# The second loop of a two-layer network: loop heads in the middle of the work, and more of the dense expert ahead of the triangular solve

## The chip, the cores and the metric

The program runs on one core of one Trainium2 chip. The metric is the device time of one launch, in microseconds (us), as the median of several runs. Names of the engines: PE is TensorE (matrix products and transposes), DVE is VectorE, ACT is ScalarE, POOL is GpSimd, SP is the engine that issues transfers. A PE product of float32 operands is issued as two passes; "x8" in a row of the profile counts passes.

## What is computed

The input is 8 batches of 512 tokens with 128 features. Two layers run one after the other; each normalises its input and adds an attention-like block and a mixture of experts to it. The change touches the second layer only:

```
xn = layernorm(x)
x  = x + L1_attn_ref(xn, ...) + L1_ffn_ref(xn, ...)

L1_attn_ref:
    x = zrms(hidden, w_ln1);  qkvz = x @ W_qkvz;  q, k, v, z = split(qkvz)
    b, a = split(x @ W_ba);   beta = sigmoid(b);  g = -exp(A_log) * softplus(a + dt_bias)
    q, k, v = silu(causal_dwconv([q, k, v], conv_w))          # 4 taps, 2048 channels
    step: S = S * exp(g);  S = S + k (v - k S) beta;  o = q S  # over 512 tokens, 8 heads of 128 x 128
    core = rms(o) * gate_norm_w * silu(z);  h = resid + core @ W_out
    h + sum over the top 2 of 8 small experts of (silu(gate) * up) @ down
L1_ffn_ref:
    probs = softmax(x @ w_router);  top 2 of 8 experts
    out = sum_e probs_e * (gelu(x @ w1_e + b1_e) @ w2_e + b2_e)   # hidden width 512, all 8 experts computed
```

The recurrence over tokens is computed in four chunks of 128 tokens. For each chunk and head a 128 x 128 unit lower triangular system is inverted: first its 32 x 32 diagonal blocks, all of them at once, by substitution (this is the triangular solve), then the larger blocks by products.

## The kernel before, in words

A first loop of 8 iterations computes layer one for each batch, a second loop of 8 iterations (one batch each, b) computes layer two. In the second loop every engine runs its own instruction stream. One list, `schedule_l1`, gives the order of steps; each engine walks through it and emits what it has to do for a step, or nothing. Semaphores order the engines among each other, and within an engine the order of the list is kept strictly. The names of the steps:

- `qkv m` projects channel blocks m and m+1 (PE, L692) into banks 2 to 5 of PSUM and ACT copies them to the ring CV of four (L1014); `taps m` are six multiply-adds on DVE (L1519) with the older taps; `silu m` (ACT, L1021) writes the activated block and for m below 8 its square (L1026); `ssq m` sums the squares on PE (L716). Block m+4 needs the ring place of block m: its copy waits for that block's silu, its product for that block's taps.
- `gg`, `gc`: decay rates on DVE (L1498), their sums on PE (L700), a copy on DVE (L1504), and SP sends it to DRAM and back in four broadcasts (L418, L422) for `scan` (DVE, L1531). `stat` makes scales (L1536), `gam` exponentials (ACT, L1030, L1033) and products (POOL, L1165). `prep c` makes key products (PE, L729, banks 0 and 1 in turn) and multiplies them by the decays (DVE, L1562). `stat2` (L1549 to L1553) makes more scales, `wfT` transposes the dense router's weights (PE, DVE copy L1508).
- `sub 0` to `sub 3`: the triangular solve, 31 steps of two operations on DVE (L1575, L1577), each waiting for the one before. Then SP writes the result to DRAM and reads it back in another layout; `inv` (PE, ACT, DVE, POOL L1175) builds the larger blocks.
- `cz c`: the z projection (PE, L737, banks 0 and 1) and its silu (ACT, L1040); for c of 2 and 3 the result is stored over the solve's memory. `cv c`: v transposed and scaled (ACT, L1053).
- The dense expert: 32 steps f, four for each of 8 experts e. `fh f` (PE, L871) makes a 128 x 512 block of the hidden layer in PSUM bank HBANK[f], `gelu f` (ACT, L1100), `fo f` (PE, L881) adds its product to bank OBANK[e], and `facc e` (DVE, L1684) takes the finished expert out of that bank, so that the bank can be used again. Where HBANK is the same for f and f+1, `fh f+1` waits for `gelu f`.
- Steps of the tail: `moe1 p` are the four pairs of small experts (L921, L923, L927; DVE L1729, L1733; their down product L915, and `moe1_last`, L1739). Among them the next batch is begun: `gn`, `gx`, `gz`, `gT`, `gr`, `gzT`, `gba`, and `gend`, which makes the gates (L1482 to L1487) and the router's top 2 (L1447 to L1490) on DVE and their exponentials on ACT (L997 to L1003).

Ahead of the loop the tail's part for the first batch is emitted once. Each engine's loop head lies at the start of the list, between `gend` and `qkv 0`. The lines that set the placement of the dense expert:

```
HBANK = (7, 4, 5) + (7,) * 17 + (2,) * 12
OBANK = (6, 3, 6, 3, 6, 3, 5, 3)
```

## Time and profile before

| | us |
|---|---|
| median of 3 runs (3119.16 to 3141.93) | 3121.79 |
| the profiled execution, whole | 3141.66 |
| its span in the trace | 3139.9 |
| PE busy, weight loads busy | 2691.1, 1805.5 |
| DVE, ACT, POOL busy | 2042.6, 1185.7, 382.3 |

The first loop ends at about 1160 us of the span; the second fills the rest. The profiled execution was 20 us longer than the median. A row of the timeline reads: start in us, duration in us, engine, source line, operation, tensors written and read, shapes, count, and in brackets how long the engine had been idle before it and what ended that. PEclk is the clock granted to PE as a share of full speed; it has the levels 1.0 (2.4 GHz) and 0.5 (1.2 GHz). `arena` is the name of nearly all of the working memory and `bank` that of all PSUM banks, so a row is identified by its line.

### The profile page before, as it was taken

What the parts mean: (1) busy time and instruction counts of PE and PEld (TensorE: products, weight loads), DVE (VectorE), ACT (ScalarE), POOL (GpSimd) and SP (SyncE); (2) the same over time, 40 slices, a digit from 0 to 9 for tenths busy, and PEclk for the clock granted to TensorE, in tenths of its full rate; (3) what the DMA queues carried; (4) which work ended last, traced back from release to release, by engine and by line L of the source; (5) the groups of instructions that cost most, each with busy time, mean ns of one, the idle gap of its engine ahead of it and who ended that gap; (6) DMA issues with size and microseconds to landing.
All of it is one profiled execution on the core that took longest, in us unless ns stands there. A gap on an engine that the chain in (4) does not pass through costs nothing.

```text
span 3139.9 us, 48523 instructions
## 1 busy us (share of the span) xinstructions
PE 2691.1 (86%) x15020; PEld 1805.5 (58%) x15020; DVE 2042.6 (65%) x6346; ACT 1185.7 (38%) x2170; POOL 382.3 (12%) x284
## 2 busy tenths in 40 slices
PE   2888888888888867997997897898898898898898
PEld 1434343343433425784785685585596595586587
DVE  4757666585766748558558557657656756845845
ACT  0132231313223125445445444444444444544543
POOL 0000000000000002122112122021120220221211
PEclk8888878897898967998998998997998898899799
DMA  5020101102011121101101101101201201100110
GB/s 139 10 38 7 33 14 25 35 5 37 12 28 21 18 51 41 48 11 58 48 11 58 48 11 49 57 8 48 61 1 55 54 8 55 43 19 28 54 34 15
DMA packets 133697, 109.63 MB, mean 35 GB/s; under 512 B 76968, under 2 KB 117488, under 8 KB 132944
## 3 DMA queue, kind: packets, MB, share of 16 engines
q1 hardware_dynamic: 130192, 100.01, 12.7%
q10 hardware_dynamic: 3264, 6.82, 0.6%
q8 instruction: 100, 1.64, 0.2%
q14 instruction: 141, 1.16, 0.1%
HBM read 86.62 MB, written 20.19 MB: 34 GB/s over the span
## 4 chain that ended last, share of the span: by engine, by line
PE 62%; issue 18%; DVE 11%; DMA 3%; ACT 3%; SPq 2%; POOL 1%; DVEq 0%; ACTq 0%; POOLq 0%
PE bank L871 7%; PE bank L881 7%; PE bank L459 5%; DMA arena<-scrk 3%; DVE arena L1519 3%; PE bank L716 2%; PE bank L610 2%; PE bank L737 2%; PE bank L819 2%; PE bank L555 2%; PE bank L782 2%; PE bank L777 2%; PE bank L765 2%; PE bank L540 2%; PE bank L769 2%
## 5 line engine op out<-in xcount | busy, mean ns | idle before, releaser
L881 PEld LDWEIGHTS bank<-wring,arena 128*128 128x128 f32 x2048 | 269.1, 192 | 109.5 <-issue 107.2
L871 PE MATMUL bank<-arena,wring 128*128 128x512 f32 x512 | 294.8, 666 | 25.9 <-ACT arena L1100 25.9
L1100 ACT ACTIVATE arena<-bank,w_b 128x512 f32<-128x512 f32 x256 | 175.1, 687 | 274.2 <-PE bank L871 273.9
L1519 DVE SCALAR_TENSOR_TENSOR arena<-bank,w_convw,arena 128x511 f32<-128x511 f32 (+2 forms) x384 | 254.8, 740 | 34.6 <-ACT arena L1014 34.5
L881 PE MATMUL bank<-wring,arena 128*128 128x128 f32 x2048 | 271.1, 276 | 0.0
L973 ACT ACTIVATE arena<-bank 128x512 f32<-128x512 f32 x136 | 81.4, 599 | 494.7 <-PE bank L540 441.9
L459 PE MATMUL bank<-w_ident,arena 128*128 128x128 f32 (+2 forms) x1164 | 178.5, 293 | 86.4 <-DVE arena L1266 35.7
L1372 DVE CUSTOM_DVE_ANT_0 bank<-bank,arena 128x128 f32<-128x128 f32 (+3 forms) x512 | 249.2, 492 | 0.0
L982 ACT ACTIVATE arena<-bank 128x512 f32<-128x512 f32 (+1 forms) x384 | 171.1, 535 | 148.9 <-PE bank L597 147.1
L459 PEld LDWEIGHTS bank<-w_ident,arena 128*128 128x128 f32 (+2 forms) x1164 | 135.9, 141 | 118.6 <-issue 66.6
L692 PE MATMUL bank<-arena,w_Wqkvz 128*128 128x512 f32 x256 | 152.7, 733 | 45.0 <-DVE arena L1519 26.1
L1066 ACT ACTIVATE arena<-bank 128x512 f32<-128x512 f32 (+1 forms) x256 | 118.7, 488 | 136.2 <-PE bank L777 69.3
L570 PE MATMUL bank<-arena 48*128 48x128 bf16 (+3 forms) x512 | 110.7, 317 | 64.7 <-DVE arena L1372 36.0
L555 PE MATMUL bank<-arena 128*128 128x128 f32 x1088 | 161.7, 293 | 2.7 <-DVE arena L1357 2.7
L1684 DVE SCALAR_TENSOR_TENSOR arena<-bank,arena 128x128 f32<-128x128 f32 x224 | 63.1, 344 | 154.5 <-PE bank L881 152.7
L540 PE MATMUL bank<-arena 128*128 128x512 f32 x272 | 156.3, 659 | 8.1 <-ACT arena L973 8.1
L326 DVE TENSOR_TENSOR tick<-nhalf 128x1 f32<-128x1 f32 x600 | 94.1, 157 | 93.0 <-PE bank L570 86.4
L543 PE MATMUL bank<-arena 128*128 128x512 f32 x272 | 152.2, 644 | 0.0
L570 PEld LDWEIGHTS bank<-arena 48*128 48x128 bf16 x512 | 34.1, 93 | 200.5 <-DVE arena L1372 92.3
L555 PEld LDWEIGHTS bank<-arena 128*128 128x128 f32 x1088 | 135.6, 196 | 22.8 <-issue 11.3
L1175 POOL TENSOR_TENSOR arena<-arena,w_blk 128x512 f32<-128x512 f32 x64 | 79.8, 1268 | 509.5 <-PE bank L765 358.8
L1165 POOL TENSOR_TENSOR arena<-arena 128x512 f32<-128x512 f32 x64 | 92.3, 1475 | 352.2 <-ACT arena L1033 224.6
(273 smaller groups left out, 5209.3 us busy)
## 6 DMA issues: line engine op xcount, KB each, us to landing
wring<-in_w_last SPq DMA_DIRECT2D x64, 512.0 KB, 3.3
arena<-scrg SPq DMA_DIRECT2D x32, 512.0 KB, 5.4
arena<-scrq SPq DMA_DIRECT2D x108, 64.0 KB
arena<-scrk SPq DMA_DIRECT2D x108, 64.0 KB
scrn<-arena SPq DMA_DIRECT2D x64, 64.0 KB, 1.9
arena<-scrn SPq DMA_DIRECT2D x8, 512.0 KB, 3.6
scrx<-arena SPq DMA_DIRECT2D x8, 512.0 KB, 2.6
arena<-scrx SPq DMA_DIRECT2D x64, 64.0 KB, 2.1
```

Source lines behind the costliest of these rows:

```text
L459: return nc.tensor.transpose(dst, src, W["ident"][0:k, 0:k])
L540: mm(bk[:, :], W["gate0"][:, p, :] if p < PR0 else W["sg"][:], xnT, start=True, stop=True).then_inc(*s["p_gate"].up)
L543: mm(bk[:, :], W["up0"][:, p, :] if p < PR0 else W["su"][:], xnT, start=True, stop=True).then_inc(*s["p_up"].up)
L555: last = mm(bank[7][:, t * P:(t + 1) * P], HID[:, p % 2, t * P:(t + 1) * P], W["down0"][:, p, :] if p < PR0 else W["sd"][:], start=(p == 0 ...
L570: mm(bk[:, 0:w], QS[o:o + KROWS, h // 2, qt * P:(qt + 1) * P], KS[o:o + KROWS, h // 2, 0:w], start=True, stop=True, tile_position=(o, 0)). ...
L692: mm(bk[:, :], W["Wqkvz"][:, m * P:(m + 1) * P], zT, start=True, stop=True).then_inc(*s["p_qkv"].up)
L871: mm(bank[HBANK[f]][:, :], wring[:, e % 2, k * P:(k + 1) * P], xn1T, start=True, stop=True).then_inc(*s["p_fh"].up)
L881: last = mm(bank[OBANK[e]][:, t * P:(t + 1) * P], GH[:, f % 2, t * P:(t + 1) * P], wring[:, e % 2, FC * P + k * D:FC * P + (k + 1) * D], s ...
L982: fn(PT[:, slot, col:col + w], bank[SBANK[n % 4]][:, 0:w], ACT.Exp, scale=float(HD) ** -0.5).then_inc(*s["a_p"].up)
L1100: fn(GH[:, f % 2, :], bank[HBANK[f]][:, :], ACT.Gelu_apprx_tanh, bias=W["b1"][:, f:f + 1]).then_inc(*s["a_gh"].up)
L1372: v.tensor_tensor_reduce(bk[:, 0:w], bk[:, 0:w], W["maskq"][:, S - w:S], 1.0, PAD, ALU.add, ALU.max, mx[:, col:col + 1]).then_inc(*s["v_ma ...
L1519: ins = v.scalar_tensor_tensor(out=cv[:, k:S], in0=bank[2 + m % 4][:, 0:S - k], scalar=W["convw"][:, m, 3 - k:4 - k], in1=cv[:, k:S], op0= ...
```

## The change

**The order.** The list from `qkv 0` to the end of the solve is new, and HBANK and OBANK with it:

```diff
-HBANK = (7, 4, 5) + (7,) * 17 + (2,) * 12
-OBANK = (6, 3, 6, 3, 6, 3, 5, 3)
+HBANK = (1, 7, 7, 4, 5) + (7,) * 15 + (2,) * 12
+OBANK = (6, 6, 2, 3, 6, 3, 5, 3)
...
+    order = [("qkv", 0), ("fh", 0), ("gelu", 0), ("fh", 1), ("gelu", 1), ("taps", 0), ("gg",), ("qkv", 2), ("silu", 0)]
+    order += [("fo", 0), ("fo", 1), ("taps", 2), ("qkv", 4), ("gc",), ("silu", 2), ("taps", 4), ("ssq", 0)]
     order += [("qkv", 6), ("silu", 4), ("taps", 6), ("ssq", 2), ("silu", 6), ("scan", 0), ("ssq", 4), ("ssq", 6), ("stat",)]
...
+    order += [("scan", 1), ("fh", 2), ("fh", 3), ("fh", 4), ("gam",), ("prep", 0), ("gelu", 2), ("fo", 2), ("prep", 1), ("gelu", 3)]
+    order += [("fh", 5), ("fo", 3), ("qkv", 8), ("gelu", 4), ("prep", 2), ("gelu", 5), ("prep", 3), ("facc", 0), ("fo", 4), ("rr",)]
+    order += [("qkv", 10), ("fo", 5), ("taps", 8), ("fh", 6), ("gelu", 6), ("fh", 7), ("gelu", 7), ("taps", 10), ("silu", 8), ("fo", 6)]
+    order += [("qkv", 12), ("taps", 12), ("silu", 10), ("fo", 7), ("qkv", 14), ("taps", 14), ("silu", 12), ("silu", 14)]
+    made[:] = 8, 8
+    order += [("cz", 0), ("cz", 1), ("sub", 0)] + ffn(4) + [("sub", 1), ("facc", 1)] + ffn(3) + [("sub", 2), ("facc", 2)] + ffn(3)
+    order += [("sub", 3), ("facc", 3), ("stat2",)] + ffn(1) + [("wfT",), ("cz", 2), ("cz", 3), ("cv", 0)] + ffn(1) + ffn_rest() + [("facc", 4)]
```

Before, `fh 0` to `fh 3` stood ahead of `sub 0`, and `fh 4` to `fh 19` beside the solve with `facc 0` and `facc 1`; `wfT` and `stat2` stood between `taps 14` and `sub 0`.

**The tail.** `gend` is split in three: `gfe` (exponential and softmax of the dense router) ahead of `moe1 3`, `gab` (the gates) and `gpick` (the top 2) after it and ahead of `moe1_last`. Three small operations on beta and a move from the gates into `gg`. The down products are steps of their own, one of them placed after `gzT` and one after `gba`.

**The loop heads.** PE, ACT and DVE emit the part of the list ahead of a turning point once before the loop; the loop then holds the rest of an iteration and the first part of the next, 7 times, and the last rest follows behind it. PE turns ahead of `cz 0`:

```diff
+            turn = L1.index(("cz", 0))
+            ahead_of_loop(gT, gr, gzT, gba, first_part)
+            with pe.Fori(0, LOOPS - 1) as b:
+                second_part(b, 0)
+                first_part(b, 1)
+            out_of_loop(second_part, LOOPS - 1)
```

ACT turns in the same way ahead of `("qkv", 10)`, DVE behind `("sub", 3)`. POOL and SP keep theirs. SP loads the first two experts of the next batch at its end and no longer at its start. Some waits follow the new banks: `fo 4` waits for `facc 0`, `cz 2` for the copy of `wfT`, and `wfT` for the second silu of `cz 1`.

In the engines' own order it looks so. PE from the first key products on; bank 0 and 1 are the key products (`prep`), bank 6 is `fo`, bank 7 `fh`, bank 2 and 3 `qkv 8`. Before:

```order
L729 MATMUL bank0<-arena 128x256 x2
L676 REGISTER_ALU
L729 MATMUL bank1<-arena 128x256 x2
L676 REGISTER_ALU
L729 MATMUL bank0<-arena 128x256 x2
L676 REGISTER_ALU
L729 MATMUL bank1<-arena 128x256 x2
L876 ISA
L881 MATMUL bank6<-wring,arena 128x128 x4
L692 MATMUL bank2<-arena,w_Wqkvz 128x512
L692 MATMUL bank3<-arena,w_Wqkvz 128x512
```

and now, where the rows with bank 6 are `fo 2` and `fo 3`:

```order
L738 MATMUL bank0<-arena 128x256 x2
L738 MATMUL bank1<-arena 128x256 x2
L894 MATMUL bank6<-wring,arena 128x128 x4
L738 MATMUL bank0<-arena 128x256 x2
L738 MATMUL bank1<-arena 128x256 x2
L884 MATMUL bank7<-arena,wring 128x512
L894 MATMUL bank6<-wring,arena 128x128 x4
L700 MATMUL bank2<-arena,w_Wqkvz 128x512
L700 MATMUL bank3<-arena,w_Wqkvz 128x512
```

An output product of the dense expert now stands between the first and the second pair of key products; before, the first one stood behind both pairs.

ACT around the copies of `qkv 10` into CV; L1014 and L1042 are these copies, L1100 and L1128 the gelu, L1021 and L1049 the silu. Before:

```order
L1014 ACTIVATE arena<-bank5,w_convw 128x512
L1095 REGISTER_ALU
L1100 ACTIVATE arena<-bank7,w_b1 128x512
L1019 REGISTER_ALU
L1021 ACT_TABLE_LOAD
L1021 ACTIVATE arena<-arena 128x512
L1019 REGISTER_ALU
L1021 ACTIVATE arena<-arena 128x512
L1011 REGISTER_ALU
L1014 ACTIVATE arena<-bank2,w_convw 128x512
```

and now (the rest of an iteration behind the end of the loop):

```order
L1159 COMPARE_AND_BRANCH
L1042 ACTIVATE arena<-bank4,w_convw 128x512
L1042 ACTIVATE arena<-bank5,w_convw 128x512
L1128 ACTIVATE arena<-bank7,w_b1 128x512 x2
L1049 ACT_TABLE_LOAD
L1049 ACTIVATE arena<-arena 128x512 x2
L1042 ACTIVATE arena<-bank2,w_convw 128x512
```

Two gelus, `gelu 6` and `gelu 7`, stand ahead of `silu 8` where one stood, and the loop's branch ahead of all of them.

DVE at the end of the solve, whose steps are L1575 and L1577 before and L1630 and L1632 now; L1684 and L1739 are `facc`. Before:

```order
L1258 REGISTER_ALU
L1577 TENSOR_TENSOR arena<-arena 128x31
L1675 REGISTER_ALU
L1684 SCALAR_TENSOR_TENSOR arena<-bank6,arena 128x128 x4
L1675 REGISTER_ALU
L1684 SCALAR_TENSOR_TENSOR arena<-bank3,arena 128x128 x4
L1675 REGISTER_ALU
L1684 SCALAR_TENSOR_TENSOR arena<-bank6,arena 128x128 x4
```

and now, where L1817 is the loop:

```order
L1632 TENSOR_TENSOR arena<-arena 128x31
L1817 REGISTER_ALU
L1817 COMPARE_AND_BRANCH
L1739 SCALAR_TENSOR_TENSOR arena<-bank,arena 128x128 x4
L1604 SCALAR_TENSOR_TENSOR arena<-arena 128x32
L1605 TENSOR_SCALAR arena<-arena 128x32
L1607 TENSOR_SCALAR arena<-arena 128x16
L1608 TENSOR_TENSOR arena<-arena 128x16
L1563 COPY arena<-bank 8x512
```

Three `facc` followed the last step of the solve; now the branch, one `facc`, `stat2` (L1604 to L1608) and the copy of `wfT` (L1563) follow it, in that order.

## Rows read from the trace of the kernel before

**Rows 1.** The page's first line.

```profile
span 3139.9 us, 48523 instructions
```

**Rows 2.** The last addition of an iteration (L1739), by its line.

```profile
L1739 DVE TENSOR_TENSOR arena<-arena,bank x8: 686/689/690, 1423.5 to 3135.4; 128x512 f32<-128x512 f32 x8
```

**Rows 3.** Busy time by stretch: the solve's, and the rest to `gend`.

```profile
1733.30:1777.70 44.40, 41.28 (x193) 26.79 (x194) 28.50 (x85) 21.71 (x32) 2.50 (x2) 0.96 0.25 72
1777.70:1908.90 131.20, 127.10 (x888) 109.88 (x886) 72.88 (x237) 51.46 (x107) 25.13 (x21) 0.96 0.04 11
```

**Rows 4.** Timeline where one iteration ends and the next begins.

```profile
1663.78 0.69 DVE L1733 TENSOR_TENSOR arena<-arena,bank 128x512 f32<-128x512 f32 x1
...
1666.51 0.18 DVE L1482 TENSOR_TENSOR arena<-bank,w_dtb 128x32 f32<-128x32 f32 x1
...
1668.28 0.37 DVE L1243 MAX8 top<-pad 128x8 f32<-128x8 f32 x4
...
1668.55 5.39 PE L692 MATMUL bank<-arena,w_Wqkvz 128*128 128x512 f32 x8 [2.68 <-issue]
...
1670.69 0.69 ACT L1014 ACTIVATE arena<-bank,w_convw 128x512 f32<-128x512 f32 x1 [1.75 <-PE bank L692]
...
1673.64 4.03 DVE L1519 SCALAR_TENSOR_TENSOR arena<-bank,w_convw,arena 128x511 f32<-128x511 f32 x6 [3.56 <-ACT arena L1014]
```

**Rows 5.** Timeline of DVE at its head in the first loop.

```profile
462.70 0.68 DVE L1238 TENSOR_TENSOR arena<-arena 32x512 bf16<-32x512 f32 x1
465.69 0.69 DVE L1389 COPY arena<-bank 128x512 f32<-128x512 f32 x1 [2.30 <-issue]
```

**Rows 6.** Timeline: the decay sums leave DVE, and the scan.

```profile
1679.05 0.28 DVE L1504 COPY arena<-bank 32x127 f32<-32x127 f32 x1 [1.06 <-PE bank L459]
...
1691.06 4.55 DVE L1531 TENSOR_TENSOR_SCAN arena<-arena,w_floor 128x512 f32<-128x512 f32 x4
```

**Rows 7.** DMA issues of 1682.0 to 1682.7: median us to landing last.

```profile
arena<-scrg SPq DMA_DIRECT2D x2, 512.0 KB, 6.2
```

**Rows 8.** Timeline of the key products and the gelus beside them.

```profile
1704.35 1.28 ACT L1100 ACT_TABLE_LOAD   x1
1704.90 0.73 PEld L729 LDWEIGHTS bank<-arena 128*128 128x128 f32 x4 [3.18 <-DVE arena L1562]
...
1705.64 1.27 ACT L1100 ACTIVATE arena<-bank,w_b 128x512 f32<-128x512 f32 x2
...
1712.40 5.11 DVE L1562 TENSOR_TENSOR arena<-bank,arena 128x512 f32<-128x512 f32 x8 [2.98 <-PE bank L729]
...
1713.06 1.05 PE L881 MATMUL bank<-wring,arena 128*128 128x128 f32 x8
```

**Rows 9.** Timeline of the later taps and the silu beside them.

```profile
1717.42 15.83 DVE L1519 SCALAR_TENSOR_TENSOR arena<-bank,w_convw,arena 128x511 f32<-128x511 f32 x24
...
1720.82 1.28 ACT L1021 ACTIVATE arena<-arena 128x512 f32<-128x512 f32 x2
```

**Rows 10.** Timeline of the solve: its start, one expert step, its end.

```profile
1733.99 2.50 POOL L1175 TENSOR_TENSOR arena<-arena,w_blk 128x512 f32<-128x512 f32 x2 [20.11 <-ACT arena L1021]
1734.02 1.27 DVE L1553 TENSOR_TENSOR arena<-arena 128x16 f32<-128x16 f32 x1
...
1735.44 0.91 DVE L1569 MEMSET arena<- 128x1024 f32 x1 [0.16 <-issue]
...
1743.33 1.12 PE L871 MATMUL bank<-arena,wring 128*128 128x512 f32 x2 [1.52 <-ACT arena L1100]
...
1744.49 0.69 ACT L1100 ACTIVATE arena<-bank,w_b 128x512 f32<-128x512 f32 x1 [1.22 <-PE bank L871]
...
1762.25 1.13 DVE L1684 SCALAR_TENSOR_TENSOR arena<-bank,arena 128x128 f32<-128x128 f32 x4
1766.26 3.94 PE L737 MATMUL bank<-w_Wqkvz,arena 128*128 128x512 f32 x8
...
1777.90 1.13 DVE L1684 SCALAR_TENSOR_TENSOR arena<-bank,arena 128x128 f32<-128x128 f32 x4 [10.31 <-PE bank L881]
```

328 lines of the change are left out of this document (183 added, 145 removed).

## The prediction, made before the changed kernel was run

> **What bounds the kernel now.** I read the page's first line for the span [rows 1], then the last addition of each iteration by its line. Its eight starts lie 1711.9 us apart in seven periods, so an iteration of the second loop takes 244.6 us [rows 2]; the first loop isn't touched. Then I cut one iteration into stretches. From the inversion's products to the end PE is busy for 127 of 131 us [rows 3]: that part is PE's, and the change leaves its order alone but for the last few steps. So everything is decided between the last small expert (DVE's L1733) and the inversion's start, in three places.
>
> First, the seam between two iterations [rows 4]. DVE ends L1733 at 1664.47 and starts the first taps at 1673.64, 9.2 us later. The view names ACT's copy as what ended its last wait, but that copy was over at 1671.38, 2.3 us before. DVE's last work was over at 1670.08, and the gap behind it is 3.56 us; PE shows 2.68 us before L692 with nothing that it waited for. The same kind of gap, 2.30 us, stands at DVE's loop head in the first loop, where little else goes on [rows 5]. These are the heads.
>
> Second, the taps. From 1673.64 to 1733.25 DVE works nearly without a pause: the scan starts 17.4 us after the first taps [rows 4, 6], the last eight products of key and decay at 1712.40, and taps 8 to 14 fill 15.8 us [rows 8, 9]. DVE, not PE, sets when the solve can start.
>
> Third, the solve: DVE runs it from 1735.44 to 1762.25, 26.8 us with two `facc` in it. But the inversion starts only at 1777.7, with the last `fo`: DVE then has waited 10.31 us for PE [rows 10]. An expert step takes 0.69 + 1.22 = 1.91 us there. So PE's sixteen steps are late here, and not the solve.
>
> **The change part by part.** I write t for the time since the first taps of an iteration. Before: `taps 8` at 43.8, end of `taps 14` at 59.6, inversion at 59.6 + 44.45.
>
> *The seam.* No head is left in it. After L1733 DVE does the gates (from 1666.51, three operations, 0.6 us), the top 2 (from 1668.28 to 1670.08, 1.8 us) and the last addition (0.69 us) [rows 2, 4]: 3.1 us. ACT has two short exponentials, a table load (1.28 us [rows 8]) and a logarithm before its first copy of 0.69 us, about 3.4 us in all; PE's first product is issued right behind its last down product. I take 3.5 us, so 5.7 us are saved at each of seven seams: 39.9 us. Bounds: 2.6 (if only the head's idle 2.7 us of PE goes) and 6.1.
>
> *The decay sums.* Their copy to DRAM now stands behind `taps 2`: at t = 4.0 + 1.0 (`gg` with three more operations) + 4.0, ending at 9.3. From that copy to the last broadcast it takes 1682.2 + 6.2 - 1679.3 = 9.1 us [rows 6, 7], so the scan can't start before t = 18.4, where it started at 17.4. Cost 1.0 us (0 to 1.3). The two new gelus and their two table loads lie on ACT beside `taps 0`, and PE's `fh 0` to `fo 1` fill its pauses: 0 us.
>
> *`fo 2` between the key products.* Before, PE took up the third key product as soon as DVE freed its bank, at 1704.90 [rows 8]. Now it stands behind `fo 2`, which waits for `gelu 2`; ACT reaches that after its exponentials at 1704.35, plus 1.28 of table load and 0.64 of gelu, so 1706.3. `fo 2` then takes 0.9 us at PE's full clock and about twice that at the lower one (1.05 with its tail in [rows 8]). The third product is there at 1708.0 to 1709.7 where DVE could take it at 1706.1. Behind it the row of work (`fh 5`, `fo 3`, `qkv 8`) is as long as the one that made DVE wait 2.98 us. Cost 0.8 to 2.5 us; I take 1.5, since PE stands idle ahead of it and the clock tends to be low after that.
>
> *`facc 0` ahead of `taps 8`*: 1.13 us of DVE [rows 10], on the path. It isn't saved later, since the solve still holds two of its kind.
>
> *The copies for `taps 12`.* Let s be the start of `taps 8`. PE waits with `fo 4` for `facc 0`, that is until s; then `fo 4` 0.9, `qkv 10` 1.7, `fo 5` 0.9, `fh 6` 1.1 until its result: `gelu 6` from s + 4.7. `fh 7` has the same bank, so it follows at s + 5.5, `gelu 7` ends at s + 7.3, table load to s + 8.6, `silu 8` to s + 9.9 (1.28 [rows 9]), first copy to s + 10.6. DVE wants it at s + 8.0. What was hidden, since one gelu stood there and PE was early, is now 2.6 us late; `taps 14` has its copies in time. I take 2.9 (1.5 to 5.0; the upper end is PE at its lower clock).
>
> Sum up to the end of `taps 14`: 1.0 + 1.5 + 1.15 + 2.9 = 6.55 us later in t, in each of eight iterations: 52.4 us lost.
>
> *The solve and what follows it.* From the end of `taps 14`: the solve 26.8 us at once (the copy and `stat2` are gone from its front). POOL's two products, 1.25 us each, fall beside its first steps instead of beside `stat2`, where one small operation of 16 columns took 1.27 [rows 10] and one of 32 columns elsewhere takes 0.18 [rows 4]; 1.1 us (0 to 2.5). Then DVE's head, 3.0 us (2.3 [rows 5] to 3.6 [rows 4]), `facc 3` 1.1, `stat2` 0.6, copy of `wfT` 0.7: 33.3. Only then may `cz 2` start: both `cz` 4.6 us until their last silu, `cv 0` 1.6, table load 1.3, `gelu 19` 0.7, `fo 19` 0.9, pauses 0.6: 43.0 where it was 44.45. PE's eleven steps from `fh 8` end at about 26, so the four that were taken out of this stretch gain little: DVE's late head takes PE's place. Gain 1.45 us, eight times 11.6; the first and the last iteration have no head there, 2 x 3.0 = 6.0 more. Bounds per iteration: 3.5 gained, 2.5 lost. The heads of PE (before `cz 0`, which must wait for ACT's `silu 14` anyway) and ACT (before `qkv 10`, where it idles) I cost at nothing; without that cover each would be some 3 us.
>
> SP's two loads at the end of an iteration are transfers of the next experts 0 and 1, wanted only behind `qkv 0`, and are issued 20 us ahead: 0.
>
> Sum: 52.4 - 39.9 - 11.6 - 6.0 = -5.1 us. The profiled execution would take 3136.6; it was 20 us above the median, so I put the forecast at 3121.8 - 5 = 3117 us.
>
> **Two rules of the Trainium skill.** The page "Advanced Engine Details and Errata", section Control Flow Timing, gives about 108 ns for a compare-and-branch; "Runtime: NRT & Kernel Launch", section Instruction fetch mechanics, says that a taken branch to a target outside the fetched window stalls. The gaps of 2.3 to 3.6 us stand with the second. The page "SBUF — State Buffer", section on its two sides, says that a DVE operation with two SBUF inputs and a GpSimd operation exclude each other for a whole instruction; by that all of POOL's 2.5 us would be lost to the solve, and the sum would be an estimated +6 us in place of -5.
>
> **Rivals.** (a) The placements are absorbed: `fo 2` and the copies for `taps 12` come in time, because PE and ACT run earlier against DVE than I count. For it: ACT is busy for 28.5 of 44.4 us in the solve's stretch and for 51.5 of 131.2 behind it [rows 3], so it has room. Against: both orders are strict, and the steps were counted from rows. Without the 1.5 and the 2.9 us the sum is -5.1 - 35.2 = -40: 3081 us; with the solve's part at its better bound, 3062.
> (b) Slower: PE's lower clock. PE now stands still ahead of `fo 4` and for six us ahead of `cz 2`; in the kernel before, the eight passes of L692 behind a pause of 2.68 us took 5.39 us [rows 4], where those of `cz` behind another took 3.94 [rows 10]. If each of the two chains pays 2.5 us more, in every iteration, the sum is +35 us: 3157. It decides from about 4.5 us an iteration on.
> (c) The seam's gap isn't the head but something else that stays, as a branch of 0.1 us would have it. Then each seam saves 3.5 us less (+24.5) and DVE's turn after the solve costs nothing (-18): +1.4, 3123.
>
> **How the numbers follow.** Forecast 0.45, (a) 0.30, (b) 0.20, (c) 0.05. The forecast's own range is 3092 to 3150, from its bounds taken half together. 1% is 31 us, about what can be told from no change. Faster by more: 0.30; within: 0.50; slower by more: 0.20. The range over the cases is 3070 to 3158.
>
> **What would show it.** After: seven seams of 3.5 us from DVE's last L1733 to the first taps; no idle of 3 us there on PE. A wait of about 2.6 us of DVE before `taps 12`, ended by ACT's copy. Before the third key product, PE waiting for a gelu. After the solve an idle of 3 us on DVE, then PE waiting some 6 us for the copy of `wfT`, and no 10 us wait of DVE for the last `fo`. It is wrong if the seam saves under 4 us, or if DVE's taps run through without a gap.

## The result, and the profile after

The changed kernel took 3171.09 us (median of 4 runs, 3168.62 to 3178.63), the kernel before 3126.78 us beside it (3119.16 to 3141.93): a ratio of 1.014, 95% interval 1.0095 to 1.0184. A second measurement, on one chip with three of the experiments, gave 3175.54 us against 3139.60 us, ratio 1.011 (1.0071 to 1.0148). The change makes the kernel slower by 1.1 to 1.4%. The forecast of 3117 us had the wrong sign, and 3171 lies above its range, which ended at 3158. The two profiled executions that are compared below are 30 us apart (3141.66 and 3172.09), the medians 44 us and 36 us: the profiled execution of the kernel before was as long as the longest of its four runs, though near the medians of its later ones.

The page of the changed kernel, first the span and then the busy times of the engines:

```profile
span 3170.3 us, 48083 instructions
...
PE 2686.2 (85%) x15020; PEld 1806.1 (57%) x15020; DVE 2045.0 (65%) x6343; ACT 1205.0 (38%) x2194; POOL 382.0 (12%) x284
```

PE and DVE have as much to do as before (2691.1 and 2042.6). Only ACT has more, 1205.0 us where it had 1185.7, with 138 loads of its function table of 1.28 us each, where it had 114. The span is 30.4 us longer than that of [rows 1]. So on PE and DVE the change added waiting and not work. The last additions of the iterations, by their line, tell how much of it an iteration takes (they answer to [rows 2]):

```profile
L1794 DVE TENSOR_TENSOR arena<-arena,bank x8: 678/681/683, 1436.7 to 3166.7; 128x512 f32<-128x512 f32 x8
```

Seven periods take 3166.7 - 1436.7 = 1730.0 us, so 247.1 us for an iteration where it was 244.6. The measure for all experiments below is this period, since the first loop, which the change leaves alone, differs from one profiled execution to the next: the first taps of the second loop start at 1188.3 us in the kernel before, at 1194.5 in the changed one, and between 1183.8 and 1209.7 in the experiments. A kernel's own period differed by 0.4 to 0.6 us between its two profiled executions (runs 8 and the changed kernel), so smaller differences than that tell nothing.

**The seam.** The timeline of the changed kernel at the end of an iteration, as in [rows 4]; L1788 is the last small expert, L1794 the last addition, L1574 the taps:

```profile
1682.07 0.69 DVE L1788 TENSOR_TENSOR arena<-arena,bank 128x512 f32<-128x512 f32 x1
...
1683.99 1.88 PE L700 MATMUL bank<-arena,w_Wqkvz 128*128 128x512 f32 x4
...
1684.93 0.68 DVE L1794 TENSOR_TENSOR arena<-arena,bank 128x512 f32<-128x512 f32 x1
...
1685.83 4.17 DVE L1574 SCALAR_TENSOR_TENSOR arena<-bank,w_convw,arena 128x511 f32<-128x511 f32 x6 [0.22 <-ACT arena L1042]
```

From the end of L1788 at 1682.76 to the first taps at 1685.83 it is 3.1 us, where it was 9.2. PE starts the next projections, without a pause, while DVE still picks the top 2. This part of the change does what was expected.

**The key products.** The timeline from `prep 0` to `prep 2` of that iteration; L1617 is DVE's product of key and decay, L894 `fo`, L738 the key products, L1128 the gelu:

```profile
1716.94 2.45 DVE L1617 TENSOR_TENSOR arena<-bank,arena 128x512 f32<-128x512 f32 x4
1717.05 0.63 ACT L1061 ACTIVATE arena<-arena 128x512 f32<-128x512 f32 x1 [1.28 <-DVE arena L1586]
1717.70 1.28 ACT L1128 ACT_TABLE_LOAD   x1
1719.00 1.26 ACT L1128 ACTIVATE arena<-bank,w_b 128x512 f32<-128x512 f32 x2
1719.74 2.08 PE L894 MATMUL bank<-wring,arena 128*128 128x128 f32 x8 [5.49 <-ACT arena L1128]
...
1723.56 1.29 DVE L1617 TENSOR_TENSOR arena<-bank,arena 128x512 f32<-128x512 f32 x2 [4.16 <-PE bank L738]
...
1729.84 5.00 DVE L1617 TENSOR_TENSOR arena<-bank,arena 128x512 f32<-128x512 f32 x8 [3.28 <-PE bank L738]
```

PE waits 5.49 us for `gelu 2`, then needs 2.08 us for eight passes that took 1.05 in [rows 8], and DVE stands still for 4.16 us where it had worked on. The later wait of 3.28 is the old one of 2.98. The gelu itself comes when the prediction said, 2.7 us after the start of DVE's first product of key and decay (1719.63 after 1716.94; forecast 1706.3 after 1703.59). In the mean of eight iterations DVE's products of key and decay take 17.5 us from start to end, 12.6 before.

**The later taps.** The same iteration; L1737 is `facc 0`:

```profile
1734.75 1.12 DVE L1737 TENSOR_SCALAR arena<-bank,arena 128x128 f32<-128x128 f32 x4
...
1736.01 2.05 PE L894 MATMUL bank<-wring,arena 128*128 128x128 f32 x8 [2.50 <-DVE arena L1737]
...
1740.40 4.23 DVE L1574 SCALAR_TENSOR_TENSOR arena<-bank,w_convw,arena 128x511 f32<-128x511 f32 x6 [0.60 <-ACT arena L1042]
...
1748.03 7.96 DVE L1574 SCALAR_TENSOR_TENSOR arena<-bank,w_convw,arena 128x511 f32<-128x511 f32 x12 [3.40 <-ACT arena L1042]
```

In [rows 9] the 24 operations of `taps 8` to `taps 14` ran in one piece. Now there are waits of 0.60 and 3.40 us in them, for ACT's copies. PE ran `fo 4` in 2.05 us again, not in 1.05.

**The solve, its start.** DVE's first steps (L1630, L1632) and POOL's two products (L1221), which fell on `stat2` in [rows 10]:

```profile
1756.16 0.91 DVE L1624 MEMSET arena<- 128x1024 f32 x1 [0.16 <-issue]
1756.74 2.49 POOL L1221 TENSOR_TENSOR arena<-arena,w_blk 128x512 f32<-128x512 f32 x2 [29.51 <-ACT arena L1049]
...
1757.29 0.76 DVE L1630 TENSOR_TENSOR arena<-arena 128x31 f32<-128x31 f32 x1
1758.08 1.19 DVE L1632 TENSOR_TENSOR arena<-arena 128x31 f32<-128x31 f32 x1
1759.30 0.22 DVE L1630 TENSOR_TENSOR arena<-arena 128x60 f32<-128x60 f32 x1
```

**Its end.** L1739 is `facc 3`, L1563 the copy of `wfT`, L748 `cz 2` and `cz 3`, the last row the last `facc` ahead of the inversion:

```profile
1787.43 1.12 DVE L1739 SCALAR_TENSOR_TENSOR arena<-bank,arena 128x128 f32<-128x128 f32 x4 [2.88 <-issue]
...
1788.82 0.67 DVE L1563 COPY arena<-bank 8x512 f32<-8x512 f32 x1
...
1789.55 5.82 PE L748 MATMUL bank<-w_Wqkvz,arena 128*128 128x512 f32 x8 [6.23 <-DVE arena L1563]
...
1800.71 1.13 DVE L1739 SCALAR_TENSOR_TENSOR arena<-bank,arena 128x128 f32<-128x128 f32 x4 [11.22 <-PE bank L894]
```

DVE's head is the gap of 2.88 us that no other engine ended. PE waits 6.23 us for the copy of `wfT` behind it. `cz 2` and `cz 3` take 5.82 us where these products took 3.94 in [rows 10], and DVE waits longer for the last `fo` than before (11.22 against 10.31).

**The clock.** Busy time by stretch for five stretches of that iteration; the columns are the stretch, its length, busy us and count of PE, weight loads, DVE, ACT and POOL, then the granted clock as a share of 2.4 GHz, the DMA share and GB/s:

```profile
1718.00:1726.00 8.00, 6.26 (x18) 5.09 (x19) 3.42 (x7) 2.25 (x3) 8.00 (x5) 0.57 0.00 0
1734.00:1742.00 8.00, 5.99 (x22) 4.01 (x22) 7.29 (x15) 1.37 (x2) 0.00 (x0) 0.79 0.34 61
1755.00:1764.00 9.00, 5.82 (x7) 2.15 (x8) 8.15 (x21) 5.40 (x8) 2.49 (x2) 0.62 0.01 2
1786.00:1794.00 8.00, 4.45 (x6) 1.81 (x6) 2.06 (x9) 2.48 (x3) 0.00 (x0) 0.57 0.59 132
1810.00:1818.00 8.00, 8.00 (x44) 7.88 (x43) 1.62 (x4) 2.39 (x4) 0.00 (x0) 0.57 0.01 2
```

PE runs for most of four of them at the lower level, 1.2 GHz (0.57 and 0.62), and for some two fifths of the second (0.79). The first four hold the four long waits of PE: for `gelu 2`, for `facc 0`, for the silu ahead of `cz 1`, and for the copy of `wfT`. In the fifth PE is busy all the time: it is the inversion, ten us in, and PE is the bound there.

The kernel before is not free of this. In the iteration that the forecast read, the stretches that answer to the first four have clocks of 0.79, 1.00, 0.62 and 1.00. PE waited for the copy of `wfT` too, but ahead of the solve, and the eight passes of `cz 0` and `cz 1` behind that wait took 5.30 us. And in this iteration, though in no other of the eight, the inversion too ran at half clock for a stretch (a row of the timeline, then, in a view of its own, the stretch that answers to the fifth above):

```profile
1733.88 5.30 PE L737 MATMUL bank<-w_Wqkvz,arena 128*128 128x512 f32 x8 [6.68 <-DVE arena L1508]
```

```profile
1788.00:1796.00 8.00, 8.00 (x43) 7.88 (x43) 1.12 (x4) 2.39 (x4) 0.00 (x0) 0.57 0.01 2
```

Over the second loop, from its first taps to its last addition, PE has half clock for 335 us before and for 330 us in the changed kernel, and stands still for 211 and 243 us. So the change added no half clock in sum. It moved it: in all eight iterations of the changed kernel some of it lies in the inversion, which PE bounds, and before in one of eight. Before, most of it lay in the taps and at the start of the solve, where DVE sets the time.

### The profile page after: what moved, and what is told of

The parts are those of the page before. It is cut to its first block, busy times and chain, and to the rows that moved or that the text cites. A ratio compares the mean times of both kernels' runs of the same rounds, so it can differ in the third digit from the quotient of the medians.

```text
span 3170.3 us, 48083 instructions
## 1 busy us (share of the span) xinstructions
PE 2686.2 (85%) x15020; PEld 1806.1 (57%) x15020; DVE 2045.0 (65%) x6343; ACT 1205.0 (38%) x2194; POOL 382.0 (12%) x284
## 4 chain that ended last, share of the span: by engine, by line
PE 52%; issue 17%; DVE 16%; DMA 6%; ACT 4%; SPq 3%; POOL 1%; DVEq 0%; ACTq 0%; POOLq 0%
PE bank L470 5%; PE bank L894 4%; PE bank L884 4%; DMA arena<-scrk 4%; DVE arena L1632 3%; DVE arena L1630 3%; PE bank L830 2%; PE bank L566 2%; PE bank L793 2%; PE bank L621 2%; PE bank L788 2%; PE bank L776 2%; PE bank L551 2%; PE bank L780 2%; DVE arena L1574 2%
## 5 line engine op out<-in xcount | busy, mean ns | idle before, releaser
L894 PEld LDWEIGHTS bank<-wring,arena 128*128 128x128 f32 x2048 | 276.4, 199 | 187.1 <-issue 125.2
L894 PE MATMUL bank<-wring,arena 128*128 128x128 f32 x2048 | 283.6, 285 | 74.9 <-ACT arena L1128 54.9
L1574 DVE SCALAR_TENSOR_TENSOR arena<-bank,w_convw,arena 128x511 f32<-128x511 f32 (+2 forms) x384 | 257.2, 738 | 32.8 <-ACT arena L1042 31.8
L1128 ACT ACTIVATE arena<-bank,w_b 128x512 f32<-128x512 f32 x256 | 173.3, 687 | 252.1 <-PE bank L884 251.7
L748 PE MATMUL bank<-w_Wqkvz,arena 128*128 128x512 f32 x128 | 90.9, 861 | 93.6 <-ACT arena L1068 48.6
L1739 DVE SCALAR_TENSOR_TENSOR arena<-bank,arena 128x128 f32<-128x128 f32 x224 | 63.1, 344 | 147.0 <-PE bank L894 125.9
L566 PEld LDWEIGHTS bank<-arena 128*128 128x128 f32 x1088 | 135.9, 196 | 23.1 <-issue 12.6
L1221 POOL TENSOR_TENSOR arena<-arena,w_blk 128x512 f32<-128x512 f32 x64 | 79.7, 1267 | 574.0 <-PE bank L776 344.8
L884 PEld LDWEIGHTS bank<-arena,wring 128*128 128x128 f32 x512 | 91.1, 210 | 92.0 <-ACT arena L1128 46.7
```

The costliest lines, as they stand in the source:

```text
L566: last = mm(bank[7][:, t * P:(t + 1) * P], HID[:, p % 2, t * P:(t + 1) * P], W["down0"][:, p, :] if p < PR0 else W["sd"][:], start=(p == 0 ...
L884: mm(bank[HBANK[f]][:, :], wring[:, e % 2, k * P:(k + 1) * P], xn1T, start=True, stop=True).then_inc(*s["p_fh"].up)
L894: last = mm(bank[OBANK[e]][:, t * P:(t + 1) * P], GH[:, f % 2, t * P:(t + 1) * P], wring[:, e % 2, FC * P + k * D:FC * P + (k + 1) * D], s ...
L1128: fn(GH[:, f % 2, :], bank[HBANK[f]][:, :], ACT.Gelu_apprx_tanh, bias=W["b1"][:, f:f + 1]).then_inc(*s["a_gh"].up)
L1574: ins = v.scalar_tensor_tensor(out=cv[:, k:S], in0=bank[2 + m % 4][:, 0:S - k], scalar=W["convw"][:, m, 3 - k:4 - k], in1=cv[:, k:S], op0= ...
```

## The experiments

All times are medians; the ratio is to the kernel before, run beside it on the same chip. "Period" is the mean of seven in the profiled execution. "End of taps" is the end of `taps 14` since the first taps, "inversion" its first copy since the first taps, and "rest" from there to the start of DVE's last product for the small experts, each a mean over eight iterations. "Steps ahead" in runs 8 and 11 to 13 are steps of the dense expert moved ahead of the solve, beyond those of the kernel before.

| kernel | us | ratio (95%) | period | end of taps | inversion | rest |
|---|---|---|---|---|---|---|
| before | 3126.78 | 1 | 244.6 | 60.8 | 107.0 | 127.5 |
| changed | 3171.09 | 1.014 (1.0095 to 1.0184) | 247.1 | 69.1 | 113.5 | 129.4 |
| changed, again | 3175.54 | 1.011 (1.0071 to 1.0148) | 247.7 | 68.9 | 113.3 | 129.7 |
| 1 new heads, old order | 3110.77 | 0.988 (0.9836 to 0.9926) | 238.6 | 61.6 | 107.5 | 127.4 |
| 2 new order, heads at the start | 3160.44 | 1.004 (1.0019 to 1.0059) | 245.1 | 69.4 | 110.9 | 127.5 |
| 3 DVE's head behind `wfT` | 3156.28 | 1.003 (0.9996 to 1.0055) | 244.7 | 69.1 | 111.0 | 129.7 |
| 4 filled wait ahead of `cz 2` | 3161.22 | 1.005 (1.0027 to 1.0077) | 245.6 | 68.8 | 112.8 | 128.1 |
| 5 silu first | 3152.54 | 1.004 (1.0005 to 1.0068) | 244.4 | 66.7 | 111.8 | 128.3 |
| 6 `fo 2` behind | 3147.30 | 1.002 (0.9995 to 1.0046) | 243.8 | 66.7 | 111.5 | 127.8 |
| 7 all of 3, 5 and 6 | 3107.19 | 0.988 (0.9829 to 0.994) | 237.5 | 63.9 | 106.1 | 127.2 |
| 8 two steps ahead | 3098.69 | 0.986 (0.9794 to 0.9917) | 237.0 | 60.5 | 104.6 | 128.1 |
| 8 again | 3102.81 | 0.988 (0.9818 to 0.9942) | 237.4 | 60.4 | 104.7 | 128.3 |
| 9 old order, heads at the start | 3131.30 | 0.997 (0.9931 to 1.0005) | 242.3 | 62.0 | 108.1 | 127.8 |
| 10 four waits filled | 3125.28 | 0.995 (0.9907 to 0.9985) | 241.8 | 65.4 | 109.1 | 128.7 |
| 11 three steps ahead | 3115.55 | 0.991 (0.9873 to 0.9955) | 241.1 | 60.2 | 107.7 | 128.9 |
| 12 three steps, DVE's head late | 3085.29 | 0.982 (0.976 to 0.9884) | 235.7 | 60.1 | 103.8 | 127.9 |
| 13 two steps, DVE's head late | 3073.40 | 0.976 (0.9698 to 0.9828) | 235.1 | 60.8 | 103.8 | 127.4 |

Beside the experiments the kernel before ran 82 times more, in four groups with medians of 3146.63, 3143.23, 3139.60 and 3145.74 us and single runs from 3117.58 to 3168.43: two of the three runs behind the forecast were among its quickest. The ratios are taken within a group.

### 1 and 9: the heads and the tail without the new order

Run 1 is the changed kernel with the old list, its banks and its waits:

```diff
-    order = [("qkv", 0), ("fh", 0), ("gelu", 0), ("fh", 1), ("gelu", 1), ("taps", 0), ("gg",), ("qkv", 2), ("silu", 0)]
+    order = [("qkv", 0), ("taps", 0), ("gg",), ("qkv", 2), ("silu", 0), ("gc",), ("taps", 2), ("qkv", 4), ("silu", 2), ("taps", 4), ("ssq", 0)]
...
-HBANK = (1, 7, 7, 4, 5) + (7,) * 15 + (2,) * 12
-OBANK = (6, 6, 2, 3, 6, 3, 5, 3)
+HBANK = (7, 4, 5) + (7,) * 17 + (2,) * 12
+OBANK = (6, 3, 6, 3, 6, 3, 5, 3)
```

> The changed kernel with the list from qkv 0 to the solve, HBANK, OBANK and the waits that go with them as they were before; heads, tail and loads of the first experts as changed. The trace after shows 6.9 us less at each of seven seams. Theory H (the heads pay, the order costs): the DVE head behind sub 3 falls into DVE's wait of some 10 us for the last fo, the others into idle time too, so the gain is about 7 x 6.9 = 48 us: 3079 us where before takes 3127, and no half clock behind the inversion's start. Rival R (a head costs wherever it stands, and the half clock comes from the peeled loop, not from the order): 3120 to 3160 us, with DVE late behind the solve.

Run 9 has the three turning points at the start of that list besides:

```diff
-            turn = L1.index(("cz", 0))
+            turn = 0
...
-            turn = L1.index(("qkv", 10))
+            turn = 0
...
-            turn = L1.index(("sub", 3)) + 1
+            turn = 0
```

> The old order as in the run with the new heads alone (238.6 us an iteration), but all three turning points at the start of the list: the changed tail by itself. With the new order the same edit cost 2.9 us at each seam (6.7 instead of 3.8 from the last product of the small experts to the first taps; 9.85 before the change). Theory: half of what the seam gained came from the split of the gates and the top 2 in the tail and half from the heads: seam 6.7, iteration 241.5 us, ratio to before 0.988 + 0.007 = 0.995. Rival: the heads were worth all 6.1 us: seam 9.8, iteration 244.6.

Run 1 took 238.6 us an iteration, 5.9 less than before, and 8.5 less than the changed kernel. So the heads and the tail together are the gain, and the order, with its banks and waits, is the whole loss: it costs 8.5 us an iteration, and what the heads and the tail win covers 5.9 of it. The last additions of run 1, by their line:

```profile
L1788 DVE TENSOR_TENSOR arena<-arena,bank x8: 680/680/681, 1436.8 to 3107.2; 128x512 f32<-128x512 f32 x8
```

Run 9 took 242.3 us. From the last product of the small experts to the first taps (start to start) it is 9.85 us before, 6.37 in run 9 and 3.76 in run 1. So of the 6.1 us that the seam gained, 3.5 come from the split of the gates and the top 2 in the tail and 2.6 from the heads: near the theory that was put down for run 9, and not its rival. By the whole period the tail gave 2.3 us and the heads 3.7. In run 1 DVE's head stands behind the solve too (3.06 us of idle time that no engine ended), and still the inversion starts 107.5 us after the first taps, 107.0 before: the copy of `wfT`, which PE wants, is ahead of the solve there.

### 2 and 3: where DVE's head stands

Run 2 is the changed kernel with the three turning points at the start of the list, as in run 9. Run 3 moves one of them:

```diff
-            turn = L1.index(("sub", 3)) + 1
+            turn = L1.index(("wfT",)) + 1
```

> The changed kernel with all three turning points at the start of the list, so the heads of PE, ACT and DVE lie between gpick and qkv 0 again. Theory H: seven seams longer by 6 us (+42), DVE's 2.9 us behind the solve saved seven times (-20), and PE then waits 3.3 us and not 6.2 ahead of cz 2, which may or may not bring the clock back (0 to -39): 3154 to 3193 us where the changed kernel takes 3171. Rival R (the heads' places are indifferent): 3171 within 5.

> The changed kernel with only DVE's turning point moved from behind sub 3 to behind the copy of wfT, where DVE waits 11.2 us for the last fo. Theory H: cz 2 starts 2.9 us earlier in seven iterations, 20 us, and the head costs nothing where it stands: 3151 us. If PE's shorter wait ahead of cz 2 also keeps the clock up for cz 2, cz 3 and the inversion's first products, up to 39 us more: 3112. Rival: the last fo sets the inversion anyway: 3171.

In run 2 the seam is 2.9 us longer and the inversion starts 2.6 us earlier since the first taps; the rest is 127.5 us and not 129.4, so the period is 245.1, 2.0 less than with the heads in their new places. In run 3 the inversion starts 2.5 us earlier and the period is 244.7, 2.5 less. In this order the head behind `sub 3` costs nearly what its gap is (2.88 us). Run 3 has both gains and still is not faster than the kernel before. Its "rest" is 129.7, as in the changed kernel, so the shorter wait ahead of `cz 2` (3.4 us and not 6.2; `cz 2` starts 2.2 us earlier) did not bring the clock back. The further 39 us of the expectation did not come.

### 4 and 10: is it the waits or the clock?

Run 4 gives PE five products in its wait for the copy of `wfT`, run 10 gives it products in four waits. Nothing reads their results.

```diff
                         if c == 2:
+                            if i == 0:
+                                need("a_sz", 4)
+                                for _ in range(5):
+                                    mm(bank[1][:, :], W["Wqkvz"][:, 0:P], W["Wqkvz"][:, 0:4 * P], start=True, stop=True)
                             need("v_wfT", 1)
```

> The changed kernel with five extra products of 128 x 512 on PE in its wait for the copy of wfT ahead of cz 2; their result in bank 1 is overwritten and never read. They fill 4.7 of 6.2 us and add no work elsewhere. Theory C (PE's standing still ahead of cz 2 brings the half clock in cz 2, cz 3 and the inversion's first products): cz 2 and cz 3 take 4.0 us again and not 5.8, and the stretch from the inversion's start to the last addition 129.7 and not 132.5 us: 8 x 4.7 = 38 us less, 3133. Rival (the half clock there follows from something else, or only shifts): 3171 within 10, with the half clock as before.

> The changed kernel with extra products of 128 x 512 in four of PE's waits: five ahead of fo 2, two ahead of fo 4, five ahead of the second product of cz in the wait for silu 14, five ahead of cz 2. Their results lie in banks 2, 7, 7 and 1, are overwritten and never read. Theory C (PE's standing still is what brings the half clock): the stretches at half clock at t = 32 to 39, 49 to 53, 70 to 77, 101 to 108 and 125 to 132 shrink or vanish, cz 2 and cz 3 take 4.0 us instead of 5.7, the inversion's start to the last product of the small experts 127.4 instead of 129.4, and the taps end 2 to 3 us earlier: 241 us an iteration instead of 247.1. Rival (the waits alone cost, the clock only follows them): 247 or more, since some of the extra products end after the wait that they fill.

Run 10 adds 69 us to PE's busy time (2755.6 against 2686.2) and in its profiled execution, the longest of its ten, takes 5.8 us less an iteration than the changed kernel beside it (241.8 against 247.7), a ratio of 0.995 where that has 1.011. Its busy time by stretch, for the five stretches that answer to those above (the same times since the first taps; same columns):

```profile
1725.00:1733.00 8.00, 6.78 (x33) 4.86 (x33) 3.62 (x6) 2.81 (x5) 8.00 (x5) 1.00 0.11 19
1741.00:1749.00 8.00, 7.14 (x30) 3.92 (x29) 6.64 (x11) 4.42 (x6) 0.00 (x0) 1.00 0.46 140
1762.00:1771.00 9.00, 7.17 (x35) 4.65 (x35) 8.12 (x26) 4.19 (x6) 0.00 (x0) 1.00 0.01 2
1793.00:1801.00 8.00, 7.18 (x25) 3.71 (x23) 0.00 (x0) 5.17 (x10) 0.00 (x0) 0.79 0.47 107
1817.00:1825.00 8.00, 8.00 (x72) 8.00 (x71) 3.29 (x6) 2.88 (x5) 1.57 (x2) 0.98 0.00 0
```

and its last additions, by their line:

```profile
L1806 DVE TENSOR_TENSOR arena<-arena,bank x8: 680/680/683, 1448.8 to 3141.6; 128x512 f32<-128x512 f32 x8
```

The clock is up in the first three, and PE gets through 72 passes in the last where it got through 44. The end of the taps comes 3.5 us earlier, `cz 2` to its end takes 5.1 us and not 5.7. Over the second loop half clock is granted for 174 us, where the changed kernel beside it has 328. So the waits of the changed kernel cost twice: for their own length, and for the half clock of the work behind them; the second price is at least the 5.8 us an iteration that more work on the same engine gives back. It is not what the change added: the kernel before has as much half clock (335 us), and it was not run with such products, so that it may well gain by them too. How much of the 8.5 us that the order costs is clock stays open, but for the rest behind the inversion's start (see below). In run 4, with one wait filled, the period was 1.5 to 2.0 us below that of the changed kernel (247.1 and 247.7), where 4.7 were expected: the low clock in `cz 2` and in the inversion came a little later and was shorter (7.3 us of the rest at half clock, 9.4 and 9.8 in the changed kernel), but it came. What decides whether a given wait brings it, these runs don't show; in run 10 four of the eight iterations have no half clock between 30 and 110 us after their first taps, and the other four have it once there.

### 5 and 6: the two placements that make DVE wait

```diff
-    order += [("qkv", 10), ("fo", 5), ("taps", 8), ("fh", 6), ("gelu", 6), ("fh", 7), ("gelu", 7), ("taps", 10), ("silu", 8), ("fo", 6)]
-    order += [("qkv", 12), ("taps", 12), ("silu", 10), ("fo", 7), ("qkv", 14), ("taps", 14), ("silu", 12), ("silu", 14)]
+    order += [("qkv", 10), ("fo", 5), ("taps", 8), ("silu", 8), ("qkv", 12), ("fh", 6), ("taps", 10), ("silu", 10), ("qkv", 14), ("taps", 12)]
+    order += [("gelu", 6), ("fh", 7), ("gelu", 7), ("fo", 6), ("silu", 12), ("fo", 7), ("taps", 14), ("silu", 14)]
```

> The changed kernel with silu 8, qkv 12, silu 10 and qkv 14 ahead of gelu 6 and gelu 7 (fh 7, fo 6 and fo 7 follow them). In the changed kernel DVE waits 0.6 us before taps 10 and 3.4 us before taps 12 for ACT's copies. Theory: these waits go and nothing else takes their place, so the end of taps 14 comes 4 us earlier and an iteration takes 243.1 us where the changed kernel has 247.1 (mean of seven periods); ratio to before 1.014 - 0.010 = 1.004. Rival (the clock: PE stands still longer in this stretch and pays it back at half clock in cz, the dense expert or the inversion): 245 to 247 us.

```diff
-    order += [("scan", 1), ("fh", 2), ("fh", 3), ("fh", 4), ("gam",), ("prep", 0), ("gelu", 2), ("fo", 2), ("prep", 1), ("gelu", 3)]
-    order += [("fh", 5), ("fo", 3), ("qkv", 8), ("gelu", 4), ("prep", 2), ("gelu", 5), ("prep", 3), ("facc", 0), ("fo", 4), ("rr",)]
+    order += [("scan", 1), ("fh", 2), ("fh", 3), ("fh", 4), ("gam",), ("prep", 0), ("prep", 1), ("gelu", 2), ("fo", 2), ("gelu", 3)]
+    order += [("qkv", 8), ("prep", 2), ("fh", 5), ("fo", 3), ("gelu", 4), ("gelu", 5), ("prep", 3), ("facc", 0), ("fo", 4), ("rr",)]
```

> The changed kernel with fo 2 behind the second pair of key products and fh 5 and fo 3 behind the third. In the changed kernel DVE waits 4.16, 0.42 and 3.28 us among the products of key and decay; the kernel before waits once, 2.98 us. Theory: PE's wait of 5.5 us for gelu 2 no longer stands ahead of the third key product; from prep 0 to the end of prep 3 it takes 13 us again and not 17.5: 4.5 us an iteration, 242.6 where the changed kernel has 247.1, ratio to before 1.002. Rival: fo 3 and gelu 5 are later now and delay facc 0, which gives 2 us or more of it back: 245.

Run 5 took 2.7 us less an iteration than the changed kernel and run 6 3.3 us; 4.0 and 4.5 were expected. In run 5 it takes 17.1 us from `taps 8` to the end of `taps 14`, 19.8 in the changed kernel and 15.8 before: of the 4.0 us two pauses of 0.7 and 0.6 us stay, ahead of `taps 10` and behind its first operation; the one ahead of `taps 12` is gone. PE's own head, hidden in the changed kernel, shows in this run: 1.8 to 2.6 us of idle time ahead of `cz 0` that no engine ended. In run 6 the waits among the products of key and decay are 0.97, 2.19 and 0.99 us in place of 4.16, 0.42 and 3.28; the kernel before had two, 0.77 and 2.98, and not the one that the expectation names (the timeline of run 6, DVE alone):

```profile
1701.83 2.61 DVE L1617 TENSOR_TENSOR arena<-bank,arena 128x512 f32<-128x512 f32 x4 [0.97 <-PE bank L738]
1706.63 2.48 DVE L1617 TENSOR_TENSOR arena<-bank,arena 128x512 f32<-128x512 f32 x4 [2.19 <-PE bank L738]
1710.11 2.48 DVE L1617 TENSOR_TENSOR arena<-bank,arena 128x512 f32<-128x512 f32 x4 [0.99 <-PE bank L738]
```

Its `taps 12` waits longer in return (from `taps 10` to `taps 12` it is 7.9 us, 7.4 in the changed kernel). Each of the two placements alone is worth some 3 us.

### 7: the three together

> The changed kernel with the three edits together: DVE's turning point behind the copy of wfT (measured 2.5 us an iteration), silu 8 and silu 10 ahead of gelu 6 and 7, fo 2 behind the second pair of key products. If the three add up: 247.1 - 2.5 - 4.0 - 4.5 = 236.1 us an iteration, ratio to before 0.98. If the clock takes part of it back: 238 to 242. If eight steps ahead of the solve are bad in any place, it stays above the 238.6 us of the old order with the new heads.

237.5 us an iteration: 9.7 less than the changed kernel, where the three apart gave 2.5 + 2.7 + 3.3 = 8.5. With these three edits, one of which is the place of DVE's head, more than all that the order cost (8.5) is back. Eight steps ahead of the solve can be had without loss, once they don't stand between a result and the engine that wants it. But it is no gain over run 1 that can be told (0.988 both).

### 8, 11, 12 and 13: fewer steps ahead, in the places that are free

Run 8 keeps the two steps at the start of the list (`fh 0` to `fo 1`, as in the changed kernel) and puts all others where they were before, with numbers two higher and OBANK as before:

```diff
+    order += [("scan", 1), ("fh", 2), ("fh", 3), ("fh", 4), ("gam",), ("prep", 0), ("prep", 1), ("gelu", 2), ("gelu", 3), ("fo", 2)]
+    order += [("qkv", 8), ("prep", 2), ("gelu", 4), ("fo", 3), ("prep", 3), ("rr",), ("qkv", 10)]
+    order += [("taps", 8), ("fh", 5), ("gelu", 5), ("taps", 10), ("silu", 8), ("qkv", 12), ("taps", 12), ("silu", 10), ("qkv", 14)]
+    order += [("taps", 14), ("silu", 12), ("wfT",), ("silu", 14), ("cz", 0), ("cz", 1), ("stat2",), ("cv", 0), ("fo", 4), ("sub", 0)]
```

> The heads of the changed kernel with the old order (238.6 us an iteration), but fh 0, gelu 0, fh 1, gelu 1, fo 0 and fo 1 at the start of the list as in the changed kernel, and the other steps in the old places with numbers two higher: six fh and four fo ahead of the solve, fourteen fh beside it instead of sixteen. Theory: the first two cost nothing, since they lie in a stretch that waits for the decay sums, and PE, which sets the inversion's start there, has two steps of 1.9 us less: 234.8 us, ratio to before 0.974. Rival: the end of taps 14 comes later by the steps at the start, or PE's rest turns into half clock: 238 or more.

> The run with six fh and four fo ahead of the solve once more, on the same chip as its two variants: 237.0 us an iteration and a ratio to before of 0.986 as measured (interval 0.979 to 0.992).

Run 11 has one step more ahead (`fo 4`, `fh 6`, `gelu 6`, `fo 5` before `taps 14`):

> The run with six fh and four fo ahead of the solve (237.0 us an iteration), with fo 4, fh 6, gelu 6 and fo 5 moved ahead of taps 14, beside silu 12; fo 4's bank is waited for with taps 12. Theory: PE idles there and the step is free, one of 1.9 us less stands beside the solve: 235.1 us, ratio to before 0.978. Rival: gelu 6 and two table loads put off silu 14, and with it cz 0 and the steps beside the solve: 237 or more.

Run 8 took 237.0 us and 237.4 us an iteration; 234.8 was expected. The two steps at the start are free (the taps end at 60.5), and the inversion starts 2.9 us earlier than in run 1, not 3.8. Run 11 was slower than run 8, 241.1 us. Its timeline at the end of the solve, with L1737 as `facc` and L892 as `fo`:

```profile
1760.20 2.36 DVE L1737 SCALAR_TENSOR_TENSOR arena<-bank,arena 128x128 f32<-128x128 f32 x8 [2.88 <-issue]
1761.47 2.04 PE L892 MATMUL bank<-wring,arena 128*128 128x128 f32 x8 [3.73 <-DVE arena L1737]
```

PE is one step further now and needs a bank that `facc` must free, and this `facc` stands behind DVE's head. So two runs more:

```diff
-            turn = L1.index(("sub", 3)) + 1
+            turn = L1.index(("facc", 3))
```

in both, and in run 12 `facc 0` behind `sub 0` besides.

> The run with seven fh and six fo ahead of the solve (241.1 us an iteration), with DVE's turning point ahead of facc 3 instead of behind sub 3, and facc 0 behind sub 0 instead of sub 1. In that run PE waits 3.7 us for facc 2, which stands behind DVE's head, and 1.25 us for facc 0. Theory T (DVE's head behind sub 3 is what delays PE, not the three steps that were moved): both waits go, an iteration takes 241.1 - 5 = 236 us or less. Rival O (more dense expert ahead of the solve is bad by itself, by the clock or by POOL's products in the solve): 239 or more.

> The run with six fh and four fo ahead of the solve (237.0 us an iteration) with DVE's turning point ahead of facc 3, where DVE waits 9.4 us for the last fo, instead of behind sub 3, where facc 1 and facc 2 follow the head. Theory T: where PE waits for facc 1 or facc 2 now, it no longer does, 0 to 2 us less: 235 to 237. Rival O: no difference, since only the run with one step more had a wait of PE for facc 2 that counts.

Run 12 took 235.7 us, 5.4 less than run 11: the places of the head and of `facc 0` together were what broke it; the two edits were not run apart. PE's wait of 3.7 us behind the head is gone, but in the solve it still waits 1.8 to 3.1 us for another `facc`, where the expectation had both waits gone. Run 13 took 235.1 us, 2 less than run 8, and is the quickest of all: 3073.40 us, ratio 0.976 (0.9698 to 0.9828). The end of its solve:

```profile
1749.16 1.13 DVE L1737 SCALAR_TENSOR_TENSOR arena<-bank,arena 128x128 f32<-128x128 f32 x4
1751.94 1.88 PE L746 MATMUL bank<-w_Wqkvz,arena 128*128 128x512 f32 x4
1753.21 1.13 DVE L1737 SCALAR_TENSOR_TENSOR arena<-bank,arena 128x128 f32<-128x128 f32 x4 [2.92 <-issue]
...
1762.61 1.13 DVE L1737 SCALAR_TENSOR_TENSOR arena<-bank,arena 128x128 f32<-128x128 f32 x4 [8.28 <-PE bank L892]
```

The head's 2.92 us now stand behind `facc 2`, which PE wanted, and ahead of `facc 3`, behind which DVE waits 8.28 us anyway. In run 12 the solve takes 28.8 us instead of 26.9, because POOL's two products fall in it again, and the inversion starts at 103.8 us in both: what the third step may win on PE does not show. The two ratios can't be told apart. In the quickest kernel PE waits 4.6 to 6.7 us ahead of `cz 0` in every iteration and has half clock behind it, as before the change, ahead of a solve that DVE sets; it is the quickest all the same.

### The changed kernel again

> The changed kernel once more, beside the others on one chip: ratio to before 1.014 as in the first measurement (interval 1.0095 to 1.0184), 247 us an iteration. A lower ratio than 1.008 would mean that the first measurement fell on quick runs of the kernel before.

1.011 and 247.7 us: the first measurement holds.

## Why the prediction was wrong, point by point

The profiled executions differ by 31.3 us from the start of the trace to the last addition (3135.4 and 3166.7). The table has the prediction's terms beside what the two traces show; its sum was -5.1 us. The 6.2 us of the first loop are a difference between two executions and nothing that the change did.

| term | forecast, us | measured, us |
|---|---|---|
| seam, 7 times | -39.9 | 7 x (3.76 - 9.85) = -42.6 |
| start of the taps to their end, 8 times | +52.4 | 8 x (69.08 - 60.84) = +65.9 |
| from there to the inversion, 8 times | -11.6 - 6.0 | 8 x (44.43 - 46.19) = -14.1 |
| inversion to the last small expert, 8 times | 0 | 8 x (129.38 - 127.48) = +15.2 |
| first loop and first head | 0 | +6.2 |
| last product to last addition, the last time | 0 | +0.7 |

- **The seam: right in size, half right in cause.** 3.1 us are left of 9.2, forecast 3.5. But the forecast called these gaps the heads. Run 9 shows that 3.5 of the 6.1 us gained come from the split tail and only 2.6 from the heads. Rival (c), that no head is in it, falls by the same run: runs 9 and 1 differ in the turning points alone. The gaps are far above the 108 ns that the Trainium skill ("Advanced Engine Details and Errata", Control Flow Timing) gives for a compare-and-branch; the Trainium skill's other rule ("Runtime: NRT & Kernel Launch", Instruction fetch mechanics), that a taken branch outside the fetched window stalls, agrees with them.
- **The heads' covers: right for PE and ACT, right in price for DVE.** In the changed kernel PE's and ACT's show nowhere as idle time of their own. DVE's 3.0 us was 2.88 (to 3.47 in other iterations), PE's "some 6 us" was 6.23, and no more than 2.5 us an iteration came back when only this head was moved.
- **The decay sums: wrong, and harmless.** The scan starts at 18.8 us and not at 18.4; before it was 19.2 in the mean, and 17.4 only in the iteration that the forecast read. The one iteration stood for eight; their taps end between 58.7 and 62.0.
- **`fo 2` between the key products: a mis-sized term.** Forecast 1.5 us with bounds of 0.8 and 2.5; from the first product of key and decay to the end it takes 17.5 us instead of 12.6, so 4.8. The gelu came when it was said, but `fo 2` (2.08 us) and the key products behind it ran at half clock. The prediction's own arrival times, 1708.0 to 1709.7 where DVE is free at 1706.1, make a wait of 1.9 to 3.6 us; it gives no reason for bounds 1.1 us below, and took a value in their middle. DVE waited 4.16 us. Ahead of this the first product of key and decay starts 1.6 us earlier than before, where the forecast had 1.0 later; what brings that was not traced. The two terms together: forecast 2.5, measured 3.3.
- **The copies for `taps 12`: right in mechanism, too small.** A wait of about 2.6 us was forecast ahead of `taps 12` and 2.9 taken; it was 3.40, and 0.60 ahead of `taps 10`. With 3.9 us in the mean this is 1.0 us an iteration above the forecast, the largest single miss within the taps. `facc 0` costs 1.0 us, forecast 1.15.
- **The solve.** One of the signs was "no 10 us wait of DVE for the last `fo`"; the wait is 11.22 us. The prediction's own sum has it: the copy of `wfT` is done at 33.3 and the last `fo` at 43.0, 9.7 us later. POOL's products cost DVE 1.5 us (28.4 against 26.9 from the memset to the end), forecast 1.1; in return 2.0 us of `stat2` and a copy are gone from its front. `cz 2` and `cz 3` take 1.8 us longer. What was forecast as 1.45 us a time, and 6 us at both ends, came to 1.8 a time in all. The rows on POOL bear out the Trainium skill's rule ("SBUF — State Buffer", SBUF: two separate sides) that a DVE operation with two SBUF inputs and a GpSimd operation that reads SBUF exclude each other: two steps of 0.19 us took 0.76 and 1.19 us while POOL's pair ran, in run 11 two of 0.25 took 1.35 and 1.20, and the memset ahead of them took 0.91 us as ever. The loss was 1.5 us and not the pair's whole 2.5, because the pair began 0.5 us before the first step, beside the memset, and two steps of 0.19 got done in its time.
- **"That part is PE's, and the change leaves its order alone": the step that failed.** It was costed at nothing, and costs 15.2 us. The order is the same there, but PE comes to it out of a wait of 6.2 us, and in the mean 9.4 us of it run at 1.2 GHz instead of 6.4. The iterations of both kernels fall into three groups: with 3.4 us at half clock the rest takes 126.0 us, with 6.8 us 127.5 to 127.7, with 10.2 us 129.9 to 130.0; before, one of eight had 10.2, now six have. That one is the iteration that the forecast read, so its 131 us of [rows 3] were not the usual case. That half clock is what lengthens this stretch is so shown. That the wait ahead of `cz 2` brings it is shown in part: with the wait filled (run 4) the rest is 1.3 us shorter, with the heads at the start (run 2) 1.9, where the wait is 3.7 us, but with the wait cut to 3.4 us (run 3) it stays.
- **Rival (b) came nearest, its number in part by luck.** It had 0.20, put PE's waits ahead of `fo 4` and `cz 2`, and gave 3157 us on a base of 3121.8, a ratio of 1.011. The measured ratios are 1.014 and 1.011. Behind the wait for `cz 2` half clock cost 1.8 us in `cz 2` and `cz 3` and 1.9 in the rest, where (b) had 2.5; behind `fo 4` it had 2.5 more, and the copies came 1.0 us later than forecast. Another 0.8 us came from the products of key and decay, which (b) does not name, and 6.2 of the measured 31.3 us lie in the first loop. The forecast weighed (b) as a mishap on top, though its own [rows 4] showed eight passes in 5.39 us after a pause. It also misread the contrast: the 3.94 us of `cz` in [rows 10] stand behind no pause of PE, and the `cz` that does, at 1733.88, took 5.30 us. A wait of PE should have been priced with the clock from the start.
- **Rival (a) fell**: nothing was absorbed. Both orders are strict, and each cost that was counted came, but for that of the decay sums.

## What to carry to other kernels

Price a new wait of PE twice, its length and the work behind it at half clock, when a stretch that PE bounds comes next; ahead of a stretch that another engine bounds, it need not cost much: run 13, the quickest kernel, has such a wait ahead of the solve in each iteration. Put a loop's head where its engine waits, but ahead of nothing that another engine wants within the next few microseconds: behind the `facc` that frees a bank and not ahead of it. Steps that fill an engine's pause must not stand, on any of the engines that they touch, between a result and its reader: six steps ahead of the solve in free places (235.1 us in run 13) were worth more than eight (237.5 in run 7).

## What the hardware showed that was not expected

- More work on PE made the kernel quicker: 69 us of products that nobody reads, and 1.6% less time than without them.
- The gap at a loop's end behind the solve is 2.87 to 3.47 us on DVE, over all iterations of the runs that show it, and none is seen where DVE waits there for another engine anyway (runs 3 and 7).
- Two products of POOL, 2.5 us together, slow two steps of DVE to four and six times their length and leave a memset alone.
- The same kernel's iterations fall into kinds. In the changed kernel the taps end 66.6 to 66.8 us after they began in the two iterations in which PE's clock is up around `fo 4`, and after 69.1 to 70.4 us in the six in which it is low there.
